# Value products of an eight-head attention issued slot by slot instead of pair by pair

## What is computed

```python
q = _split_heads(Q @ Wq.T + bq, N_HEAD)
k = _split_heads(K @ Wk.T + bk, N_HEAD)
v = _split_heads(V @ Wv.T + bv, N_HEAD)
score = jnp.einsum('bhqd,bhkd->bhqk', q, k) / jnp.sqrt(jnp.float32(d_k))
attn = jax.nn.softmax(score, axis=-1)
out = jnp.einsum('bhqk,bhkd->bhqd', attn, v)
```

## Time and profile before

| | |
|---|---|
| median of 3 runs | 1826.79 us (1822.91 to 1831.64) |
| the profiled execution, its own time | 1836.73 us |
| its span in the trace | 1834.7 us |
| TensorE's granted clock over the span | 0.878 of full |
| matmul instructions of `weigh_values` (L1082) | 2048 (512 causal, 1536 in the cross attentions) |

### The profile page before, as it was taken

How to read it: one execution, slowest core, us unless ns; L and a number is a source line. 1 busy time by engine, 2 the same in 40 slices (tenths; PEclk the granted TensorE clock), 3 DMA queues, 4 the chain that set the end, 5 groups by cost and what they waited for, 6 DMA issues and landing times. The chain is left out here.

```text
span 1834.7 us, 31839 instructions
## 1 busy us (share of the span) xinstructions
PE 1388.5 (76%) x10614; PEld 859.6 (47%) x10630; DVE 1235.9 (67%) x4823; ACT 920.4 (50%) x2002; POOL 337.9 (18%) x360
## 2 busy tenths in 40 slices
PE   5897978872874768895455799999983995777874
PEld 2454434441763543442234456666653883443442
DVE  7888368865336768887666677677764224657887
ACT  4654357641322336655622577777751442136666
POOL 3320022112524124400021000000002333303100
PEclk9999999985996879997567799999995997679997
DMA  3230014211561012310010000000003672003300
GB/s 126 55 53 2 0 22 54 36 35 48 164 125 40 12 52 49 51 25 20 1 59 1 12 7 7 12 7 7 1 2 110 186 203 59 23 18 49 55 4 24
DMA packets 59362, 83.42 MB, mean 45 GB/s; under 512 B 8065, under 2 KB 46209, under 8 KB 58689
## 3 DMA queue, kind: packets, MB, share of 16 engines
q1 hardware_dynamic: 54208, 71.15, 15.7%
q0 software_dynamic: 4992, 10.23, 3.0%
HBM read 51.18 MB, written 9.18 MB: 33 GB/s over the span
## 5 line engine op out<-in xcount | busy, mean ns | idle before, releaser
L873 ACT ACTIVATE L_xattn_probs<-ps 128x1024 f32<-128x1024 f32 x192 | 196.5, 1024 | 73.7 <-PE ps L1066 68.9
L714 DVE TENSOR_REDUCE maxs<-ps 128x4 f32<-128x1024 f32 x128 | 156.5, 1222 | 29.7 <-PE ps L1042 29.6
L3467 ACT ACTIVATE wide_pr<-wide_sc,wide_nm 128x256 f32<-128x256 f32 x256 | 127.0, 497 | 13.3 <-DVE wide_nm L3395 12.7
L1543 POOL DMA_INDIRECT moe_xs<-normed,moe_table x92 | 87.1, 947 | 156.7 <-PE ps L1573 73.9
L1042 PE MATMUL ps<-keys,L_xattn_qs 64*128 64x256 bf16 x768 | 75.3, 274 | 53.5 <-DVE maxs L714 33.3
L1082 PE MATMUL ps<-L_xattn_probs,values 128*32 128x256 f32 x1536 | 102.8, 385 | 0.0
L708 DVE CUSTOM_DVE_ANT_0 L_xattn_masked_scores<-ps,L_xattn_maskQ 128x256 bf16<-128x256 f32 x256 | 93.1, 420 | 14.1 <-PE ps L1042 14.1
L3390 DVE COPY wide_prT<-ps 128x512 f32<-128x512 f32 x64 | 44.3, 692 | 84.5 <-PE ps L3508 84.4
L3365 DVE CUSTOM_DVE_ANT_0 wide_sc<-ps,wide_mask 128x256 f32<-128x256 f32 x256 | 93.2, 419 | 3.3 <-PE ps L3493 2.2
L1972 DVE SCALAR_TENSOR_TENSOR moe_z_sb<-ps,moe_wt,moe_a_sb 128x256 f32<-128x256 f32 x46 | 22.3, 484 | 93.4 <-ACT moe_a_sb L2003 78.5
L708 DVE CUSTOM_DVE_ANT_0 L_attn_masked_scores<-ps,L_attn_maskQ 128x128 bf16<-128x128 f32 (+1 forms) x256 | 76.0, 353 | 7.6 <-PE ps L1042 7.2
(11 more groups left out here) (625 smaller groups left out, 3604.9 us busy)
## 6 DMA issues: line engine op xcount, KB each, us to landing
moe_wt<-in_packed_experts SPq DMA_DIRECT2D x23, 707.0 KB
moe_wt<-in_packed_experts SPq DMA_DIRECT2D x23, 384.0 KB
keys<-L_xattn_k_parts SPq DMA_DIRECT2D x108, 64.0 KB
L_xattn_qs<-L_xattn_q_parts SPq DMA_DIRECT2D x108, 64.0 KB
expert_out<-moe_y SPq DMA_DIRECT2D x46, 128.0 KB
weights<-in_packed_L_xattn SPq DMA_DIRECT2D x2, 1316.0 KB, 7.2
keys<-L_attn_k_parts SPq DMA_DIRECT2D x36, 64.0 KB
L_attn_qs<-L_attn_q_parts SPq DMA_DIRECT2D x36, 64.0 KB
```

Source lines behind the costliest of these rows:

```text
L714: v.tensor_reduce(nm, ps[:, BANK_M:BANK_M + 2, :].rearrange("p j (t n) -> p j t n", t=2), AX.X, ALU.max, negate=True).then_inc(S("m_used"), 1)
L873: a.activation(probs[:, s % RING, :, :, :].rearrange("p j t n -> p j (t n)"), ps[:, BANK_P:BANK_P + 2, :], ACT.Exp, scale=HD ** -0.5)\
L1543: g.indirect_dma_start(self.xs[:, j % BUFS, h * P:(h + 1) * P], None, C.normed, bass.IndirectOffsetOnAxis(self.table[:, n:n + 1], 0))\
L3467: ins = a.activation(pr[:, s % 3, j, qt, :], sc[:, s % 2, j, qt, :], ACT.Exp, bias=nm[:, s % 2, n:n + 1], accum_out=sums[:, s % 2, n:n + 1])
```

## The change

`weigh_values` takes one slot instead of a pair. It is called in every step from 4 on, for slot `s - 4`. It makes the two heads of that slot, both halves of the keys, in four calls (eight instructions). An even slot's heads take the columns 0 to 63 of the array, an odd slot's 64 to 127. The pair's `pv_ready` is sent by the odd slot. The wait for `v_ready` and for `pv_copied` stands at the even slot. The number of products, their shapes and results stay the same. The very first call moves from step 5 to step 4 and waits for one query copy more (`q_ready` 6 in place of 5).

```diff
-                def weigh_values(g, kt):
-
-                    m, b = g // (2 * GROUPS), g // GROUPS % 2
-                    if kt == 0:
-                        pe.wait_ge(S("probs_ready"), 2 * g + 2)
-                        if g % (2 * GROUPS) == 0:
+                def weigh_values(s):
+
+                    m, b, gp = slot(s)
+                    g, odd = divmod(s, 2)
+                    pe.wait_ge(S("probs_ready"), s + 1)
+                    if not odd:
+                        if s % WINDOW == 0:
                             pe.wait_ge(S("v_ready"), m + 1)
                         if g:
                             pe.wait_ge(S("pv_copied"), g)
-                    q0 = P if causal and kt else 0
-                    for j in range(4):
-                        mm = pe.matmul(ps[32 * j:32 * j + 32, BANK_V, q0:SEQ],
-                                       V[:, m % 2 * PT + 2 * b + kt, (g % GROUPS) * 4 + j, :],
-                                       probs[:, (2 * g + j // 2) % RING, j % 2, kt, q0:SEQ],
-                                       start=kt == 0, stop=kt == 1, skip_group_check=causal,
-                                       tile_position=(0, 32 * j))
-                    if kt == 1:
+                    for kt in range(2):
+                        q0 = P if causal and kt else 0
+                        for j in range(2):
+                            h = 2 * odd + j
+                            mm = pe.matmul(ps[32 * h:32 * h + 32, BANK_V, q0:SEQ],
+                                           V[:, m % 2 * PT + 2 * b + kt, (g % GROUPS) * 4 + h, :],
+                                           probs[:, s % RING, j, kt, q0:SEQ],
+                                           start=kt == 0, stop=kt == 1, skip_group_check=causal,
+                                           tile_position=(0, 32 * h))
+                    if odd:
                         mm.then_inc(S("pv_ready"), 1)
...
-                    g, odd = divmod(s - 5, 2)
-                    if not odd and 0 <= g < SLOTS // 2:
-                        if g == 0:
-                            pe.wait_ge(S("q_ready"), 5)
-                        weigh_values(g, 0)
-                        weigh_values(g, 1)
+                    if 0 <= s - 4 < SLOTS:
+                        if s == 4:
+                            pe.wait_ge(S("q_ready"), 6)
+                        weigh_values(s - 4)
```

## The result

| | before | after |
|---|---|---|
| median | 1827.03 us (4 runs) | 1860.84 us (4 runs) |
| ratio | | 1.0199, 95% interval 1.018 to 1.0217 |
| profiled span | 1834.7 us | 1859.5 us |
| TensorE's granted clock over the span | 0.878 | 0.883 |

The changed kernel is 2% slower: the two medians differ by 33.8 us, and the interval of the ratio spans 33 to 40 us. The two profiled spans differ by only 24.8 us, since the profiled execution of before lies 10 us over its median. So the changed kernel is 17.3 us behind at the start of the stretch and only 6.96 at its end.

A forecast was written before the change was run, and what follows sets the result against it. PE and DVE, both nearly full, bound the four attentions in a ring. Terms 14.6 + 13.4 + 11.2 + 6.0 + 6.0 - 2.0 = 49.2 us on 1826.79 gave 1876 us, 2.7% slower, range 1852 to 1890.

The forecast's parts named there:

- The price of eight instructions, 1.00 us: Value products per step: eight instructions on two column tiles take four rounds, 1.00 us, not 0.50.
- The wide attention's row with two tiles: Profile row of `wide_attention`: eight instructions on two 64-wide tiles take 1.08 us, next group 1.02 us after the first.
- Even steps 0.40, 0.52, 0.41 and 0.79 us late: Scores' delay in even steps: unmasked 0.40, masked 0.52, causal 0.41, and 0.79 us where side work had made PE late.
- Nothing takes a delay back: Masked and causal attentions: PE runs without a gap, so delays stay, 14.6 us masked and 13.4 us causal.
- 0.40 kept in 28 unmasked steps: Unmasked even steps with side work behind the scores, 14 in each of 2 sublayers: all 0.40 us stays, 11.2 us.
- 30 short pairs at 0.2: Unmasked attentions, the other 15 even steps in each of 2: about 0.2 us of delay is left, 6.0 us.
- The DMA wait of the second job: Unmasked attentions: the second job's first slot waits 1.30 us for keys and queries; delays partly vanish there, -2 us.
- The ends, 6 us: Each attention's start and end: step 4 +0.4, last probability scores +0.45, last pair +0.65 us; 4 x 1.5 = 6 us.
- None is added: Waits: the change adds none; `pv_copied` repeats an earlier wait, and ACT's copy stays where it was.
- The drain: After each value-product group: changing tiling mode drains TensorE, 0.14 us; without it about 33 us in sum.
- nothing absorbed (1893): Rival: no delay is absorbed even in short pairs, 66.6 us over 128 pairs, 1893 us or more; chance 0.07.
- delays ending at each job (1845): Rival: first slots of later jobs wait and absorb delay, leaving 18 us, 1845 us; chance 0.07 for 1827 to 1852.

The follow-up runs named there:

- e2: Kernel before with two of each pair's four heads left out of the value products, a constant replacing the inverse sums: 1820.17 us against 1825.05, ratio 0.9973.
- e3: Changed kernel with only the first half of the keys in the value products, a constant replacing the inverse sums: 1799.76 us against 1825.05, ratio 0.9874.
- e4: Changed kernel with only the first head of each slot in the value products, a constant replacing the inverse sums: 1861.69 us against 1823.34, ratio 1.0199.
- e1: Kernel before with each pair's products split by key halves, first half in the even step, second in the odd: 1805.16 us against 1825.05, ratio 0.9879.

## Why the prediction was right

The direction, the mechanism and the range held: 1860.84 us in 1852 to 1890. The point, 1876, lay 15 us too high: 49.2 us were forecast, 33.8 is the difference of the medians and 35.0 comes out of the trace. The 14.2 us between forecast and trace are, up to rounding, 3.4 in the even steps, 3.2 at the ends and 7.5 in what was taken back.

- **The price of eight instructions, 1.00 us.** Measured 0.99. The wide attention's row with two tiles was the right one to trust. e2, e3 and e4 show the law behind it. A price by the number of instructions would have given e2 about 1807 us and e4 about 1810.
- **Even steps 0.40, 0.52, 0.41 and 0.79 us late.** Measured 0.37, 0.50, 0.39 and 0.77 to 0.79 in most of them. Over 116 even steps the steps of the sum give 51.2 us (13.4 + 14.6 + 58 x 0.40), the trace 47.8.
- **"Nothing takes a delay back" in masked and causal, and 0.40 kept in 28 unmasked steps.** This is the term that was mis-sized: 8 us were to be returned in all (30 short pairs at 0.2, 2 for the DMA wait), 15.5 came back. The short pairs were right: those with an odd step behind them returned 0.18 us each, 5.0 in all. The statement on masked and causal was wrong: 1.9 and 2.6 us came back there. In steps 7 and 27 of all four attentions PE had waited 0.31 to 0.61 us for ACT's exponentials, and these steps returned 3.7 us. In the first unmasked attention those waits fell from 3.4 to 1.2 us, in the causal one (L1019 on L870) from 3.3 to 1.8. Of the 14 even steps with side work in an unmasked attention only 8 kept the delay. I had read the side work from the starts of transposes and scores and had not subtracted the waits that stand between them. Some 3.9 us are left that came back in small amounts, 0.01 to 0.29 us a step. A part is that the odd step's group is itself 0.013 us shorter with two tiles than with four.
- **The DMA wait of the second job, 2.0 us.** It took back 3.0: 1.3 us in the first unmasked attention, as its row said, and 1.7 in the second, whose own row of before would have said so. It was not met in later jobs.

```profile
1685.08 0.39 PE L1042 MATMUL ps<-keys,L_xattn_qs 64*128 64x256 bf16 x4 [1.67 <-issue]
```

- **The ends, 6 us.** Measured 2.8, and 1.3 of these are the stretch at the lower clock. What is left of the steps up to 5 is 1.0 us where 1.6 (4 x 0.4) had been put. The tails gave 0.5, where 4.4 (4 x 1.1) had been put on them. In the first unmasked attention the last probability scores had waited 0.52 us for ACT's exponentials, and slot 60's products went mostly into that wait: these scores come 0.19 us later and not 0.45. The last section says why the last pair costs nothing.
- **The waits.** "None is added" was wrong for the first value products of each cross attention, which wait 0.57 us for a query copy, and right for the rest. PE's waits for ACT's copy are 1.2 us in the first unmasked attention, 1.4 before, and the copy stands 1.10 us behind the start of its products (347.40 to 348.50), 1.14 before.
- **The drain.** Told as 0.14 us a group from the rows; the table of five forms leaves 0.12 to 0.14. That a change of tiling, and no other thing between two groups, takes this time was not tried by itself, so the rows fit a drain at every change of tiling and do not show one; "the trace agrees" said too much. It is not what made the change slow: e1 has as many changes of tiling.
- **The rivals** of nothing absorbed (1893) and of delays ending at each job (1845) both missed.

The total held in part by the width of the range: the price and the place of the delay were right, and the three terms that were off all erred to the same side.

## What to carry to other kernels

In this kernel small matmuls side by side on column tiles (fp32, 128 keys, 256 moving columns) cost by the longest queue of one tile, not by their number. Count rounds per tile, and when such a group must be cut in two, cut it so that both halves still use all tiles (here by key halves, 1.2% faster than the kernel before; by heads, 2% slower). Before you fill an engine's gap, look for another row of the same kernel in which the piece already has its new shape; its duration settled this case, and halving the time with the instruction count would have misled. And when a delay is carried through many steps, subtract every wait that PE already has in them, not only the one in front of the moved work.

## What was not expected of the hardware

At the end of each attention the last two slots' groups stand next to each other, the first on tiles 0 and 1, the second on tiles 2 and 3. I had charged 0.65 us for this, as if they overlapped in one round only. The changed kernel's timeline at the end of the first cross attention:

```profile
404.51 1.06 PE L1085 MATMUL ps<-L_xattn_probs,values 128*32 128x256 f32 x8
406.14 0.41 PE L1100 MATMUL ps<-const,L_xattn_pv 128*128 128x128 f32 x2 [0.57 <-ACT L_xattn_pv L957]
406.48 1.08 PE L1085 MATMUL ps<-L_xattn_probs,values 128*32 128x256 f32 x16
```

Both groups together take 1.08 us, where one takes 1.06. All eight instructions of the first are ahead of the second's in the program. Still the weight load that carries the second slot's wait starts 0.026 us after the first load of all, and four matmuls, two of each slot, have started within 0.034 us; the next one follows 0.2 us later. So here a busy tile did not hold back instructions for another tile, over eight instructions. The split by slots costs nothing where the two groups meet; it costs where transposes and scores on other tilings stand between them.
